# Moving the caps of the decay exponents from ScalarE to GpSimd in a fused attention and mixture-of-experts kernel

## The reference, cut to what matters

```
g     = cumsum(g)                       # log of the decay, per token and value head
decay = where(i <= j, exp(g[j] - g[i]), 0)
M     = where(i < j, (beta * k) k^T * decay, 0)
T     = inverse(I + M)
attn  = (q k^T) * decay
```

## Time and profile before

| | |
|---|---|
| median of 3 runs | 1360.89 us (1359.06 to 1361.21) |
| the profiled execution's own time | 1365.93 us |
| its span, first to last instruction | 1364.1 us |
| TensorE busy | 1224.1 us (90%) |
| VectorE busy | 1038.8 us (76%) |
| ScalarE busy | 903.3 us (66%) |
| GpSimd busy | 753.5 us (55%) |
| mean granted TensorE clock | 0.973 of full speed |
| chain that ended last, by engine | TensorE 73%, VectorE 13%, issue 7%, ScalarE 4% |

### The profile page before, as it was taken

The page is one execution under the profiler, slowest core; times in us unless marked ns, Lnnn a source line. Parts: engine busy times, 40 slices in busy tenths (PEclk is TensorE's granted clock), DMA queues, the critical chain, the costliest instruction groups (busy, mean ns, idle before and its releaser), DMA issues.

```text
span 1364.1 us, 32083 instructions
## 1 busy us (share of the span) xinstructions
PE 1224.1 (90%) x11612; PEld 867.1 (64%) x11612; DVE 1038.8 (76%) x1641; ACT 903.3 (66%) x1715; POOL 753.5 (55%) x790
## 2 busy tenths in 40 slices
PE   3689999999999999999999999999875389999997
PEld 2346676766767676676767677676764146666664
DVE  5686978879797988879798887979565376566565
ACT  2668888898888889888888888888753112222221
POOL 0255666766666666657666675666655483444200
PEclk9989999999999999999999999999989589999999
DMA  3111110111101011101111010101100344354431
GB/s 109 36 56 33 32 40 25 40 33 56 33 32 41 25 41 33 56 12 53 33 33 40 25 50 23 56 9 33 37 6 24 102 139 150 124 159 145 121 102 39
DMA packets 51927, 76.17 MB, mean 56 GB/s; under 512 B 8406, under 2 KB 27256, under 8 KB 51772
## 3 DMA queue, kind: packets, MB, share of 16 engines
q1 hardware_dynamic: 51700, 73.99, 17.8%
q10 hardware_dynamic: 72, 0.14, 0.0%
HBM read 72.79 MB, written 1.32 MB: 54 GB/s over the span
## 4 chain that ended last, share of the span: by engine, by line
PE 73%; DVE 13%; issue 7%; ACT 4%; DMA 1%; POOL 1%; SPq 1%; DVEq 0%; ACTq 0%; POOLq 0%
PE bank L579 15%; PE products L534 9%; PE bank L827 9%; DVE sil L1217 8%; PE products L764 6%; PE products L750 4%; PE products L738 4%; PE bank L662 3%; PE products L633 3%; PE bank L670 3%; PE bank L642 3%; PE bank L721 2%; PE bank L598 2%; PE products L618 2%; PE bank L702 2%
## 5 line engine op out<-in xcount | busy, mean ns | idle before, releaser
L579 PE MATMUL bank<-xT,whl 128*128 128x512 f16 x1152 | 297.4, 385 | 26.3 <-DVE sil L1217 26.3
L1217 DVE SCALAR_TENSOR_TENSOR sil<-bank,cw,sil 128x510 f32<-128x510 f32 (+2 forms) x384 | 283.0, 737 | 16.1 <-ACT sil L911 12.1
L579 PEld LDWEIGHTS bank<-xT,whl 128*128 128x128 f16 x1152 | 98.9, 98 | 124.9 <-DVE sil L1217 37.9
L1102 ACT ACTIVATE kq<-vtok 128x512 f16<-128x512 f32 x94 | 58.9, 629 | 174.9 <-DVE vtok L1484 174.4
L1276 DVE CAST_PREDICATED t<-levm,bank 128x512 f16<-128x512 uint8 x192 | 136.1, 709 | 39.9 <-PE bank L662 37.2
L1484 DVE SCALAR_TENSOR_TENSOR vtok<-products,b1s,zs 128x512 f32<-128x512 f32 x94 | 70.4, 749 | 92.2 <-PE products L534 92.0
L1288 DVE CAST_PREDICATED u<-levm,bank 128x512 f16<-128x512 uint8 x192 | 135.2, 704 | 0.0
L1009 ACT ACTIVATE x<-bank 128x512 f16<-128x512 f32 x160 | 96.2, 601 | 53.9 <-PE bank L642 52.6
L1545 POOL TENSOR_TENSOR hthl<-hz,hthl 128x512 f16<-128x512 f32 x64 | 74.2, 1160 | 98.2 <-ACT hthl L1046 98.2
L1604 POOL TENSOR_TENSOR at<-kqm,ex 128x256 f32<-128x256 f32 x128 | 102.6, 806 | 27.4 <-issue 14.5
L764 PE MATMUL products<-wohl,hthl 128*128 128x256 f16 x768 | 97.4, 278 | 18.4 <-POOL hthl L1545 18.1
(11 more groups left out here) (218 smaller groups left out, 3127.3 us busy)
## 6 DMA issues: line engine op xcount, KB each, us to landing
grow<-rowsc SPq DMA_DIRECT2D x64, 256.0 KB, 3.3
wt<-wqkvz SPq DMA_DIRECT2D x16, 768.0 KB, 4.5
wt<-wm SPq DMA_DIRECT2D x47, 256.0 KB, 2.9
zs<-gsc SPq DMA_DIRECT2D x36, 256.0 KB, 3.6
wo<-wout SPq DMA_DIRECT2D x16, 256.0 KB, 3.1
zs<-gsc SPq DMA_DIRECT2D x16, 224.0 KB, 3.1
zs<-gsc SPq DMA_DIRECT2D x16, 192.0 KB, 3.3
zs<-gsc SPq DMA_DIRECT2D x18, 160.0 KB, 3.0
```

The costliest lines, as they stand in the source:

```text
L579: mm = nc.tensor.matmul(dst[:, :], whl[:, h, k, col:col + HD], xT[:, l, k, half * 512:(half + 1) * 512], start=(k == 0 and m == 0), stop=( ...
L1217: nc.vector.scalar_tensor_tensor(out=dst[:, :, late:S], in0=src[:, :, 0:S - late], scalar=cw[:, q, i, 3 - late:4 - late], in1=dst[:, :, la ...
```

## The change

The step `cap` moves from ScalarE's table of steps to GpSimd's, at the same place of the walk. It becomes an add and a min with zero, so `C_G` is written with its sign turned, and `factors` loses its scale of -1. The waits stay the same four.

```diff
-            def cap(U, v):
-                (G, b), w, q = U, parity(U), U[0][1] % 2
-                n = unit_index(U)
-                act.wait_ge(s_row[n % 2], 16 * (n // 2) + 16)
-                wait_u(act, s_nt, (G, b - 2), 1, 1)
-                wait_u(act, s_at, (G, b - 2), 2, 2)
-                wait_g(act, s_sc, G, 1, 1)
-                for c in range(2):
-                    nc.scalar.activation(ex[:, w, v, c], grow[:, w, v, c], ACT.Relu, scale=-1.0,
-                                         bias=sc[:, q, C_G, v, 2 * b + c:2 * b + c + 1]).then_inc(s_cap, 1)
...
-                nc.scalar.activation(exw, exw, ACT.Exp, scale=-1.0).then_inc(s_exp, 1)
+                nc.scalar.activation(exw, exw, ACT.Exp).then_inc(s_exp, 1)
...
-                                                   scalar=1.0, in1=zc[:].rearrange("p t h -> p h t"),
-                                                   op0=ALU.mult, op1=ALU.add).then_inc(s_gcol, 1)
+                                                   scalar=-1.0, in1=zc[:].rearrange("p t h -> p h t"),
+                                                   op0=ALU.mult, op1=ALU.subtract).then_inc(s_gcol, 1)
...
+            def cap(U, v):
+                (G, b), w, q = U, parity(U), U[0][1] % 2
+                n = unit_index(U)
+                pool.wait_ge(s_row[n % 2], 16 * (n // 2) + 16)
+                wait_u(pool, s_nt, (G, b - 2), 1, 1)
+                wait_u(pool, s_at, (G, b - 2), 2, 2)
+                wait_g(pool, s_sc, G, 1, 1)
+                for c in range(2):
+                    nc.gpsimd.tensor_scalar(ex[:, w, v, c], grow[:, w, v, c], sc[:, q, C_G, v, 2 * b + c:2 * b + c + 1], 0.0,
+                                            ALU.add, ALU.min).then_inc(s_cap, 1)
```

More of the change, by code:

```diff
@@ L1092, in end @@
                 end_of(0, i)
-            attention({"gate": gate, "evict": evict, "hi": high_weights, "silu": silu, "nexp": norm, "cap": cap, "exb": row_factors,
+            attention({"gate": gate, "evict": evict, "hi": high_weights, "silu": silu, "nexp": norm, "exb": row_factors,
                        "exp": factors, "cross": cross_, "n16": high_n, "xe": xe, "g": guess, "vn": solved,
@@ L1638, in _ @@
             attention({"cw": scale_cw, "wo": out_weights, "htl": low_output, "sq": square, "qsq": square_q, "hsum": square_sum, "eye": start_inverse, "nl": low_n,
-                       "v0s": carried, "at": attention_part, "qx": carried_part, "end": end})
+                       "cap": cap, "v0s": carried, "at": attention_part, "qx": carried_part, "end": end})
             for k in range(EARLY, NK):
```

## The result

| | before | after |
|---|---|---|
| median of 4 runs each | 1361.05 us (1359.06 to 1366.09) | 1405.24 us (1400.7 to 1407.7) |
| ratio after to before | | 1.0315, 95% interval 1.0274 to 1.0357 |
| the profiled execution's own time | 1365.93 us | 1400.7 us |
| its span | 1364.1 us | 1398.9 us |
| GpSimd busy | 753.5 us (55%) | 953.5 us (68%) |

The kernel became 44 us slower. The forecast was 6.2 us slower, with a range that ended at 1375 us: the direction was right, the size was off by a factor of seven, and the result lies far outside the range. Lines of the kernel after are 12 lower than those of before between the two places where `cap` stood (L1009 is now L997, L1328 is L1316).

A forecast was written before the change was run, and what follows sets the result against it. TensorE was busy 846.14 of 880 us in the attention, with GpSimd the engine with room. Zero for ScalarE's relief, zero for the exponential's wait and 6.2 us for the collision gave 1360.89 + 6.2 = 1367.1 us, range 1359.5 to 1375.

The forecast's parts named there:

- What is removed: ScalarE in the attention: 256 activations, 86.3 us of busy time, go away; the relief was booked at zero.
- The price of a cap: One cap on GpSimd: 0.35 us by a straight line between two rows, bounds 253 ns and some 0.52 us.
- The pairs for sequence 2: Caps in GpSimd's queue before sequence 2's exponential: its wait just hidden, up to 0.1 us a period, booked at 0.
- Rival 3: ScalarE's exponential waits for GpSimd, making `xe` late: 4(d - 0.36) us a period besides the collision, 1374.6 us; chance 0.16.
- The four caps for sequence 3: GpSimd's 1.2 us gap before `hsq`: VectorE's `nt` held about 0.14 us, absorbed by a later wait.
- The collision of `sq` and `ht`: GpSimd's delayed `sq` holds VectorE's `ht` at SBUF, TensorE's `w` 0.44 us late in 14 periods: 6.2 us.
- The rest: The remaining four caps on GpSimd, before and after `hthl`, with idle time or a TensorE wait following: zero.
- The period: One head period in the attention: 60.5 us, the same to some hundredths; growth to 60.9 us was a sign.
- The range: Whole kernel time: 1359.5 to 1375 us, for caps of 0.28 to 0.40 us, no change, and rival 3's lower part.

The follow-up runs named there:

- sequence 2 alone: Only the caps of sequence 2 (64 of 256) moved to GpSimd, against the kernel before: ratio 1.0202.
- short caps: Kernel before with only the caps of sequences 0 and 1 on GpSimd, as two multiplications (0.37 us, decays left out): 1369.66 against 1362.09 us, ratio 1.0053.
- sequences 0 and 1 together: Only the caps of sequences 0 and 1 (128 of 256) moved to GpSimd, against the kernel before: ratio 1.0002.

## Why the prediction was wrong, point by point

- *What is removed: 0.* Right. The run without caps puts the worth of ScalarE's relief at 0.04%, -0.09 to 0.16.
- *The price of a cap: 0.35 us, at most 0.52.* This is the step that failed. In the kernel the cap costs 0.71 us as a median and 0.76 in the mean. The line went through a single multiplication and a pair of them, and I took both for "the same operation" as add with min. They share the instruction and not the price. The upper bound was no bound: half of a two-input instruction's 734 ns plus a fixed part had the shape of an argument, but the row itself (734 ns, 256 columns, another operation on another number of inputs) was nearest to what came out.
- *The pairs for sequence 2: just hidden, up to 0.36 us a cap.* The mechanism was right, and so was the threshold as far as it was tried: with caps of 0.37 us the wait is hidden, with 0.71 us it isn't. Rival 3 was what happened. Its formula 4(d - 0.36) at d = 0.71 gives 1.4 us a period or 21 us; sequence 2 alone lost 27. The difference is that the second pair takes 1.83 us rather than 1.40 (0.43 x 15 = 6.4 us), since `ht` of VectorE holds its first cap.
- *The four caps for sequence 3: free, since they fall into a gap of 1.2 us.* Wrong by the price again: 4 x 0.31 = 1.24 us filled the gap, while 3.15 us overran it by 1.9. I had named `nt` as the victim; it was `hsq`, and TensorE behind it, and two ScalarE instructions. The place cost 19 us, some 10 of them seen in TensorE's wait for `hsq`.
- *The collision of `sq` and `ht`: 6.2 us.* Right as a mechanism and in size, shown with short caps: 5 to 9 us where the formula says 7.3. In the kernel after it doesn't occur, because `sq` starts so late that `ht` has started before it. The loss as a function of d was not a line that rises without end; it has an upper end, where the two pass each other. I had computed the contact at one value of d and written a formula for all.
- *The rest: 0.* Right: sequences 0 and 1 together cost 0.02%, -0.15 to 0.18.
- *The period.* I wrote that it is the same to some hundredths. In the trace before, the steady periods run from 60.2 to 60.7 us, so the growth of 0.4 us that I gave as a sign could be read from a mean of periods alone. Nothing in the sum rested on it.
- *The range.* It took its top from d = 0.42. With an honest upper bound for an operation that no row shows (the 734 ns of the nearest row), rival 3 would have reached 15 x 1.5 = 22 us and the places of sequence 3 would have come into question.

## What to carry to other kernels

Price an instruction by a row with the same operation, not only with the same engine, shape and type; where there is none, take the dearest near row as the upper bound and work out each place at that value too. An engine with 45% of idle time isn't free: what counts is the gap at each place against the work put in there, and who stands behind it in the queue. On GpSimd a moved instruction also moves its later meetings with VectorE's instructions, so an order that is repaired in one place has to be looked at again in the others. Held time on an engine is a lead and not a loss: the same held `whl` cost nothing in one run.

## What the runs showed of the hardware that I had not expected

- GpSimd's `tensor_scalar` costs 0.38 us at 128x128 with two multiplications, 0.71 us with add and min, 0.72 with two additions and 0.60 with a single operation; at 128x512 it is 0.69 with two multiplications against 1.99 us with add and min.
- VectorE, waiting for its turn at SBUF behind a GpSimd instruction, can be passed over if GpSimd's next instruction follows at once: 2.05 us for an instruction of 0.69 (0.94 when it gets its turn), with starts that differ by hundredths of a microsecond. It happened in 9 of 14 periods.
- It also goes the other way: GpSimd is held by VectorE's two-input instructions. `nl` took 1.62 instead of 1.16 us behind `ht`, and `hsq` 1.73 instead of 1.27 behind `nt`.
